# Placing the SBUF tensors that TensorE reads for dense products at multiples of 128 bytes

## The reference, cut to what matters

```python
xn = layernorm(x)
# attention block (16 heads, key width 16, value width 32)
a  = rmsnorm(xn, ln1_w)
q, k, v, g = a @ Wq, a @ Wk * scaling, a @ Wv, a @ Wg + bg
gk = log_sigmoid(a @ Wkg1 @ Wkg2 + bkg2) / 16
def step(S, inp):                       # a scan over the tokens
    S = S * exp(gt)[..., None] + kt[..., None] * vt[..., None, :]
    ot = einsum('bhk,bhkd->bhd', qt, S)
o  = silu(g) * normalized(o)
y  = xn + o @ Wo
y2 = rmsnorm(y, ln2_w)
s  = y + silu(y2 @ W1) * (y2 @ W3) @ W2     # hidden width 1408 = 11 * 128
# gate block (8 low-rank experts)
alpha = softmax(relu(xn @ fW1 + b1) @ fW2 + b2)
gate  = silu(sum_k alpha_k * U_k (V_k xn))
out = x + s * gate
```

## The kernel before

| tensors | read by PE as | start | modulo 128 |
|---|---|---|---|
| `ident` | identity of transposes | 16512 | 0 |
| `causal`, `avg32`, `avg_all`, `ones` | constants | 17056 to 18592 | 32 |
| `row0`, `row1`, `row2` | inputs of transposes | 19136 to 35520 | 64 |
| `a_wk`, `a_wq`, `a_wg`, `a_wo` hi and lo | stationary, dense | 43712 to 101056 | 64 |
| `a_wv` hi and lo | moving, dense | 60096, 68288 | 64 |
| `a_wkg1`, `a_wkg2` | stationary | 109248, 110016 | 64 |
| `m_w0` to `m_w4` (same bytes as the above) | stationary, dense | 43712 to 92864 | 64 |
| `a_fold` (holds the turned keys, `kt_sb`) | stationary, small | 111136 | 32 |
| `m_xs`, `a_xa`, `f_w1` hi and lo | moving (`m_xs`, mostly `a_xa`), stationary (`f_w1`) | 120448, 128640 | 0 |
| `m_h0`, `m_h1` hi and lo | moving, dense | 136832 to 142976 | 0 |
| `m_w5` to `m_w10` | stationary, dense | 149120 to 210560 | 0 |
| `f_vt`, `f_ut` hi and lo | stationary, dense | 145024 to 194176 | 0 |
| `f_xn`, `f_vx` hi and lo | moving, dense | 161408 to 210560 | 0 |
| `a_soft`, `a_lv64`, `a_lv32`, `a_dk` | transposed, or stationary, small | 153216 to 165504 | 0 |
| `a_qx64`, `a_qx32`, `a_qxd`, `a_a0`, `a_a1` | moving, small | 169664 to 190144 | 64 |
| `a_state0`, `a_state1` | stationary, small | 194240, 196288 | 64 |
| `a_sq`, `a_og` hi and lo | moving | 198336, 204480, 212672 | 64 |
| `a_v_tok` | stationary and moving, small | 220864 | 64 |

## Time and profile before

### The profile page before, as it was taken

How to read it: one execution, slowest core, us unless ns; L and a number is a source line. 1 busy time by engine, 2 the same in 40 slices (tenths; PEclk the granted TensorE clock), 3 DMA queues, 4 the chain that set the end, 5 groups by cost and what they waited for, 6 DMA issues and landing times.

```text
span 1620.7 us, 30581 instructions
## 1 busy us (share of the span) xinstructions
PE 1593.2 (98%) x12274; PEld 1277.6 (79%) x12274; DVE 847.3 (52%) x1311; ACT 567.2 (35%) x982; POOL 167.2 (10%) x190
## 2 busy tenths in 40 slices
PE   7999999999999999999999999999999999999998
PEld 5777888777777777777777788888888888888886
DVE  5565455367797887978876451331415142241413
ACT  4333343366564645636564411111111111111111
POOL 4770000100220102101020000000000000000000
PEclk9999999999999999999999999999999999999999
DMA  7563332101020210202213423030301203030200
GB/s 175 151 135 78 83 95 69 59 27 52 9 84 0 84 53 32 84 0 84 84 54 118 144 101 127 0 136 0 136 0 49 87 0 136 0 136 0 91 14 26
DMA packets 50700, 113.16 MB, mean 70 GB/s; under 512 B 13321, under 2 KB 24665, under 8 KB 42466
## 3 DMA queue, kind: packets, MB, share of 16 engines
q1 hardware_dynamic: 47906, 99.95, 19.5%
q10 hardware_dynamic: 1152, 8.39, 1.3%
q0 software_dynamic: 1600, 4.25, 0.9%
HBM read 78.98 MB, written 33.59 MB: 69 GB/s over the span
## 4 chain that ended last, share of the span: by engine, by line
PE 94%; DVE 2%; ACT 1%; issue 1%; DMA 1%; PEld 0%; SPq 0%; ACTq 0%; DVEq 0%; PEldq 0%
PE m_ps L1529 10%; PE m_ps L1531 10%; PE m_ps L1530 10%; PE a_ps L160 7%; PE a_ps L162 7%; PE a_ps L161 7%; PE f_ps L160 5%; PE f_ps L162 5%; PE f_ps L161 5%; PE m_ps L1543 5%; PE m_ps L1544 5%; PE m_ps L1545 5%; PE a_att L1282 3%; PE a_ps L1399 2%; PE a_ps L1303 2%; PE a_ps L1390 1%
## 5 line engine op out<-in xcount | busy, mean ns | idle before, releaser
L1529 PE MATMUL m_ps<-m_xshi,m_w 128*128 128x512 f32 x680 | 268.1, 394 | 1.4 <-DVE m_w L1520 1.4
L1766 DVE TENSOR_TENSOR m_h<-m_ps,m_silu 128x512 f32<-128x512 f32 x85 | 58.7, 690 | 402.4 <-PE m_ps L1531 402.4
L1531 PE MATMUL m_ps<-m_xshi,m_w 128*128 128x512 f32 x680 | 266.5, 392 | 0.0
L1530 PE MATMUL m_ps<-m_xslo,m_w 128*128 128x512 f32 x680 | 266.4, 392 | 0.0
L1830 ACT ACTIVATE m_silu<-m_ps 128x512 f32<-128x512 f32 x85 | 50.8, 597 | 334.3 <-PE m_ps L1531 334.3
L1529 PEld LDWEIGHTS m_ps<-m_xshi,m_w 128*128 128x128 f32 x680 | 127.7, 188 | 30.0 <-issue 2.1
L1531 PEld LDWEIGHTS m_ps<-m_xshi,m_w 128*128 128x128 f32 x680 | 127.6, 188 | 28.7
L1530 PEld LDWEIGHTS m_ps<-m_xslo,m_w 128*128 128x128 f32 x680 | 127.7, 188 | 28.1 <-issue 0.2
L1101 POOL TENSOR_TENSOR row<-row,a_r 128x512 f32<-128x512 f32 x32 | 50.7, 1615 | 331.6 <-DMA a_r<-scratch_r 331.6
L1022 DVE TENSOR_TENSOR a_a<-a_att,causal 128x1024 f32<-128x1024 f32 x64 | 75.2, 1216 | 11.8 <-PE a_att L1282 11.8
L1839 ACT ACTIVATE m_h0hi<-m_h 128x512 fp32r<-128x512 f32 x46 | 29.1, 632 | 135.7 <-DVE m_h L1766 135.7
(11 more groups left out here) (306 smaller groups left out, 3487.9 us busy)
## 6 DMA issues: line engine op xcount, KB each, us to landing
row<-scratch_xn SPq DMA_DIRECT2D x16, 1024.0 KB, 4.9
row<-scratch_xmid SPq DMA_DIRECT2D x16, 1024.0 KB, 7.3
m_xt<-in_L_attn_W SPq DMA_DIRECT2D x33, 256.0 KB, 3.2
f_xt<-in_L_attn_x SPq DMA_DIRECT2D x32, 256.0 KB, 8.1
scratch_xn<-row SPq DMA_DIRECT2D x8, 1024.0 KB, 9.0
scratch_gate<-row ACTq DMA_DIRECT2D x8, 1024.0 KB, 3.9
scratch_xmid<-row SPq DMA_DIRECT2D x8, 1024.0 KB, 3.9
row<-scratch_gate SPq DMA_DIRECT2D x8, 1024.0 KB, 10.5
```

Source lines behind the costliest of these rows:

```text
L1529: pe.matmul(ps, wh, xh, start=k == 0, stop=False)
L1530: pe.matmul(ps, wh, xl, start=False, stop=False)
L1531: ins = pe.matmul(ps, wl, xh, start=False, stop=k == LAST)
L1766: dve.tensor_tensor(h[n], dense.region(f"b{j}"), silu[n], ALU.mult).then_inc(dense.taken_sem(f"b{j}"), 1)
```

## The change

Nothing is computed otherwise, and no instruction is added, taken away or moved on any engine: the lists of instructions are the same before and after, but for the addresses of their operands.

- The two small tensors `bkg2` and `bg` (32 bytes each with rounding) are allocated ahead of `wk` and no longer behind `wkg2`. They take the 64 bytes up to the next multiple of 128, so all of `wk`, `wq`, `wv`, `wg`, `wo`, `wkg1`, `wkg2` start at 0 modulo 128. `fold` and `mean` come ahead of `ln1`: `fold` goes from 32 to 0. From `ln2` on the addresses are those of before.
- `decay` and `last` (32 bytes each) are allocated behind `v_tok` and no longer ahead of `qx64`: all tensors from `qx64` to `v_tok` come down by 64 bytes, to 0 modulo 128.
- In stage m a tensor `pad` of 64 bytes comes ahead of `w0`: `m_w0` to `m_w4`, `m_r2` and the two `m_silu` go up by 64 bytes, the weights to 0 modulo 128. The tensor `room` behind them shrinks by as much, and all that follows stays.

After it every dense product has both operands at 0 modulo 128. `row0` to `row2` (64) and the constants (32) stay. The sum of the bytes in use is the same.

```diff
-    w = {name: [sb(name + part, [P, KT, n], F32R) for part in ("hi", "lo")]
-         for name, n in (("wk", KD), ("wq", KD), ("wv", D), ("wg", D), ("wo", D))}
+    w = {name: sb(name, shape) for name, shape in (("bkg2", [P, KD // P]), ("bg", [P, KT]))}
+    w.update({name: [sb(name + part, [P, KT, n], F32R) for part in ("hi", "lo")]
+         for name, n in (("wk", KD), ("wq", KD), ("wv", D), ("wg", D), ("wo", D))})
...
-    for name, shape in (("bkg2", [P, KD // P]), ("bg", [P, KT]), ("ln1", [P, KT]),
-
-                        ("fold", [P, D // 32, 16]), ("mean", [P, D // 32]),
+    for name, shape in (("fold", [P, D // 32, 16]), ("mean", [P, D // 32]), ("ln1", [P, KT]),
...
-        decay, last = sb("decay", [P, GR * NC]), sb("last", [P, GR * NC])
...
         v_tok = sb("v_tok", [P, NC, D])
+        decay, last = sb("decay", [P, GR * NC]), sb("last", [P, GR * NC])
...
+        sb("pad", [P, 16])
         w = [sb(f"w{j}", [P, 3, 2, KT, P], F32R) for j in range(5)]
```

## The result

| | before | after |
|---|---|---|
| median, us | 1624.89 (11 runs) | 1627.39 (11 runs) |
| lowest to highest, us | 1623.22 to 1627.58 | 1625.66 to 1630.33 |
| ratio of the two, 95% interval | | 1.0018 (1.0010 to 1.0026) |
| the profiled execution, us | 1622.4 | 1630.19 |
| its span, us | 1620.7 | 1628.3 |

1610.8 us was forecast, with a range of 1606.5 to 1615.5. The kernel became 2.5 us slower. Both intervals lie above 1, so the sign is sure; together they allow 0.5 to 4.2 us.

What follows compares the result with a forecast made beforehand. PE, busy 98% of the span, was taken as the bound through its dense 512-column matmuls. Savings of 8.3 us in stage m and 5.2 in stage a, 13.5 together, gave a median of 1610.8 us, range 1606.5 to 1615.5.

Steps and rivals of the forecast that it cites:

- The step that failed: Dense matmuls of stages m and a: operands unlike modulo 128 cost 6.67 ns a matmul, 2.9%, in stage m.
- `o` goes from both at 64 to both at 0, nothing: Output product of stage a: already at the fast 226.7 ns, so moving `decay` and `last` was costed at nothing.
- Stage m's sum: Pad ahead of `m_w0`: 9.6 + 0.5 - 1.1 - 0.7 = 8.3 us saved over 8 rows.
- the wait at the row's end: Stage m, transposes after block 0's up groups: DVE sets the moment, so 0.16 us at 7 row ends is lost, 1.1 us.
- Stage a's sum: `bkg2`, `bg` ahead of `wk`: faster `k`, `q`, `u`, `g`, `v` save 0.7 us a row, 5.2 us in all.
- the wait at the third chunk: Stage a, line 1399 starting behind DVE's masks: the 0.13 us a row gained by `u` and `q` is given back.
- the terms given back: Gains expected to become waits in stages m and a; the range's faster end, 1606.2 us, counted them as 2.2 us.
- The small products: Stage a, lines 1282, 1399 and 1390: changed placing taken as 0; 1282 and 1399 bounded by 2.4 us either way.
- Rival C: Stage a's small products hinder each other when operands all start at 0, so the kernel slows to 1631 us; chance 0.02.
- B, only stage m's half: DVE paces stage a, so its 5.2 us become waits and only stage m's 8.3 us arrive: 1616.0 us; chance 0.05.
- Rival A: Low-SBUF weights with high moving operands cause blocks 0 to 4's slow pace, so nothing changes: 1624.3 us; chance 0.06.
- The rule that stood beside A: PE's SBUF reads: independent ports and free weight loading make weight placement cost nothing, so 13.5 us become 0.

Runs made afterwards that it cites:

- e4_only_og: Kernel before with only `decay` and `last` moved as in the change, so `og` and `wo` start unlike; 1629.03 us against 1627.06, ratio 1.0012.
- e8_after_og_back: Changed kernel with 128 bytes ahead of `qx64`, so `og` starts like `wo` modulo 256; 1625.4 us against 1625.49 for the kernel before, ratio 1.0001.
- both sweeps: e2 and e3: kernel before with gaps giving each of `m_w0` to `m_w4` its own difference from the moving operand; 1620.9 and 1624.48 us, one run each.
- e6_after_lift: Changed kernel with everything from `m_xs` up lifted 128 bytes, dense operands at 0 modulo 256; 1613.53 us against 1625.49 for the kernel before, ratio 0.9931.
- e1_alike512: Kernel before, everything from `m_xs` up lifted 64 bytes, `decay` and `last` moved; dense operands at 192 modulo 512; 1618.05 us against 1627.06, ratio 0.9943.
- e2: Kernel before with gaps putting `m_w0` to `m_w4` 96, 160, 192, 256, 0 from the moving operand modulo 512, `wo` and `og` 256 apart; 1620.9 us.
- e3: Kernel before with other gaps, putting `m_w0` to `m_w4` 320, 384, 448, 480, 32 from the moving operand modulo 512; 1624.48 us, one run.
- e7: Kernel before with only the pad ahead of `m_w0`, blocks 0 to 4 going from 64 to 128 apart; 1624.89 us against 1625.49, ratio 0.9999.

## Why the prediction was wrong

**The step that failed** is the sentence "So it isn't the 64 that costs but that the two operands differ modulo 128; after the change they never do in a dense product". Its first half was right in that the difference of the two starts sets the pace. The modulus was not in the rows. In the kernel before the dense operands stood only at 128 and 192 modulo 256, so (leaving out the parts of `wkg1`) every pair that was alike modulo 128 was alike modulo 256 as well, and every unlike pair was unlike by both. The rows fitted 128, 256 and 512 equally well, and the prediction took the modulus that the edit's own numbers suggested. The address table held all that was needed to see it: 43712 and 120448 differ by 64 modulo 256, and after the edit 43776 and 120448 differ by 128. A rival "alike modulo 256" would have given the sign: no gain for blocks 0 to 4 or `k`, `q`, `u`, `g`, and a loss for `o`.

**"`o` goes from both at 64 to both at 0, nothing"** is the same error where it costs most. `o` was alike modulo 256 (192 and 192) and is 128 apart now: 0.26 us in 39 matmuls. `e4_only_og` shows it alone, at a difference of 64 (a row 0.31 us longer), and `e8_after_og_back` takes it back alone (0.21 us).

**The paces** were read rightly: 233.1 to 233.3 for 64 apart and 226.7 for alike, in long groups, stood in every experiment. The pace of `v` (229.1 ns, costed apart) was a hint that went unused. It differs from `g` by the same 64 bytes the other way round (192 instead of 64 modulo 256), and differences of 192 gave 229 ns again in both sweeps. A dependence on the direction says that the rule is not simply "alike or not".

**Stage m's sum** was right for the condition it meant. With all operands alike modulo 256, a row of stage m takes 91.94 us instead of 93.00, 1.06 shorter, where 1.1 was named; the wait at the row's end grew by the 1.1 us forecast; from the last `o` product to the last row's transposes (874.09 to 1613.07 us before, 873.40 to 1604.52 in `e6_after_lift`) it is 7.9 us, where the sum had 8.3.

**Stage a's sum** was too large even for that condition: 0.34 us a row (66.39 to 66.05) instead of 0.7. The term for `g` was mis-sized: 0.31 forecast, 0.10 had, since 0.18 us of it became the wait for ACT line 1183 that the earlier trace rows could not show. `v` gave 0.08 us in 35 matmuls (8.02 to 7.94). `k` gave 0.13 of its 0.16. `u` was costed at 0.05 and gave nothing (240 to 243 ns a matmul before, 242 in `e6_after_lift`), as its four differences stay the same four; the address in the table hid that. `q` gave 0.05 instead of 0.16, and the wait at the third chunk grew by 0.02 instead of 0.13; so the matmuls gained less there than thought, rather than losing it at the mask. They stand in groups of 12 between short products. In one such group of `e6_after_lift` the second starts at 585.97 us and the twelfth at 588.28: 2.31 us for ten distances, 231 ns. After short products the first six to ten matmuls run at 224 to 236 ns even with like operands, which leaves little of a group of 12 to gain. In all, 12.0 us of the 13.5 came once the operands were really alike (`e6_after_lift`; 9.0 in `e1_alike512`).

**The range** has a slip that decides nothing: the terms given back add to 1.1 + 0.7 + 7 x 0.13 + 0.3 = 3.0 us, not 2.2, so its own reckoning would begin 0.8 us lower.

**The small products** were costed at 0 between bounds of 2.4 us, and 0 it is. The 128 matmuls of the keys by queries last 1.69 us in at least 28 of the 32 chunks of every kernel of the study, and the 32 of line 1399 last 1.06 or 1.08. Rival C is out. For line 1390 the change made the operands alike modulo 256 (moving 128, stationary 192 before and 128 after), and yet its 8 matmuls of 128 columns stand 0.78 us from the first start to the last in every chunk, before, after and in `e8_after_og_back`, where they differ by 128. So the rule of the long matmuls doesn't show in these short ones. B, only stage m's half, had a piece of truth for operands that are really alike: half of stage a's gain does not arrive. **Rival A** gave the nearest time, 1624.3, by a reason that `e1_alike512` refutes: the region isn't the cause, the remainder is, only by another modulus. The rule that stood beside A, the Trainium skill, TensorE: Matmul & The Clock Gate, Part 2 (two independent read ports, and weight loading that takes nothing from the running matmul), is not borne out as the prediction used it, that the place of the weights costs nothing: moving the weights alone by 32 to 480 bytes moved the pace of a stream between 226.7 and 234 ns. Whether it is the weight load that slows the running matmul, no run separates.

**The chances.** 0.93 for faster rested on three agreeing places in one trace. They agreed because they all had the same two remainders. Three rows of the same two settings are one observation of the rule.

## What to carry to other kernels

Read starts modulo 256, and put stationary and moving operand of a long float32r product at the same remainder; which remainder (0, 128 and 192 were tried) made no difference to the pace. Only matmuls of 512 columns were seen to gain; those of 128 columns in line 1390 kept their time. Aligning one side to a round number can undo a pair that was alike by luck, so list the pairs before and after the edit, not the tensors. And when a rule is taken from a trace, ask which other rules the same rows allow: if the trace holds only two settings, it says that they differ and not by what law.

## What the runs showed of the hardware

Pace of a stream of 128x512 float32r matmuls, each with a 128x128 weight load, by the difference (stationary minus moving start) modulo 256, at a granted clock of 1.00:

| difference | ns | from |
|---|---|---|
| 0 | 226.7 | before, `o` and blocks 5 to 10; `e1`, `e2`, `e6` blocks in the low part |
| 32 | 232.5 | `e3` block 4 |
| 64 | 233.3 | before, blocks 0 to 4; `e3` block 0 (320); `e4`, `o` |
| 96 | 234 | `e2` block 0 |
| 128 | 231.7 to 233.3 | after; `e7`; `e8`; `e3` block 1 (384) |
| 160 | 232.5 | `e2` block 1 |
| 192 | 229 | before, `v`; `e2` block 2; `e3` block 2 (448) |
| 224 | 232.5 | `e3` block 3 (480) |

The rows of one block (32, 96, 160, 224) come from 12 matmuls and are good to about 1 ns. There is one fast setting, one that costs a third of the penalty, and six within 2.5 ns of each other. The runs show the table, not what makes it; weight load and stream run at the same time, so that both read SBUF together is a likely but only argued reason. The Trainium skill, SBUF — State Buffer, Specifications (TRN2), gives lines of 16 bytes and a penalty for crossing them. All starts here are multiples of 32, so by that all eight would cost the same; no run here starts an operand inside such a line, and a period of 256 is something else. The pace also has a memory: after an unlike group or a few short products, six to ten matmuls run between 224 and 236 ns before 226.7 holds.
